# Attention and expert kernel: score pairs as a stream, each side operation behind one pair alone

## The reference

```python
def attn(x, wq, wk, wv, wo):                         # layer 1, 16 heads, d = 8
    Q, K, V = rope(heads(x @ wq.T)), rope(heads(x @ wk.T)), heads(x @ wv.T)
    p = softmax(where(causal, Q @ K.T / sqrt(8), -inf))
    return merge(p @ V) @ wo.T

def ffn(x):                                          # layer 2
    x = x + msa(ln1(x))                              # full attention
    z = ln2(x)
    e = argmax(z @ gate_w + gate_b)
    return x + gelu(z @ w1[e]) @ w2[e]

x = layernorm(x + attn(x)); x = layernorm(x + ffn(x))
```

## Time and profile before

| what | value |
|---|---|
| median of three runs | 973.14 us |
| the profiled execution, its own time | 974.19 us |
| its span, first to last instruction | 972.4 us |
| PE busy, matmuls | 847.0 us, 87% |
| PE busy, weight loads | 371.3 us, 38% |
| ACT busy | 779.5 us, 80% |
| DVE busy | 326.8 us, 34% |
| POOL busy | 223.4 us, 23% |
| granted TensorE clock, mean | 0.935 |
| from the first to the last exponential | 41.9 to 873.6 us |

### The profile page before, as it was taken

How to read it: one execution, slowest core, us unless ns; L and a number is a source line. 1 busy time by engine, 2 the same in 40 slices (tenths; PEclk the granted TensorE clock), 3 DMA queues, 4 the chain that set the end, 5 groups by cost and what they waited for, 6 DMA issues and landing times.

```text
span 972.4 us, 24141 instructions
## 1 busy us (share of the span) xinstructions
PE 847.0 (87%) x9744; PEld 371.3 (38%) x9744; DVE 326.8 (34%) x957; ACT 779.5 (80%) x901; POOL 223.4 (23%) x359
## 2 busy tenths in 40 slices
PE   5689998999999999999989999889999899992261
PEld 2334434344443444333434434434444334442031
DVE  3712614311421034210323322533331633325562
ACT  2468788899999999999989989889989799890340
POOL 4741211111111100000032342033431313321253
PEclk9788999999999999999999999999999999996575
DMA  7975210201110434500100002010000000000101
GB/s 264 274 217 140 88 45 2 88 1 46 45 45 1 101 75 134 172 1 2 45 29 2 2 2 67 7 39 2 3 13 18 29 12 2 2 13 16 38 1 38
DMA packets 34355, 51.58 MB, mean 53 GB/s; under 512 B 4032, under 2 KB 14656, under 8 KB 34240
## 3 DMA queue, kind: packets, MB, share of 16 engines
q1 hardware_dynamic: 32704, 46.30, 16.6%
q0 software_dynamic: 1536, 3.67, 1.2%
HBM read 29.12 MB, written 20.84 MB: 51 GB/s over the span
## 4 chain that ended last, share of the span: by engine, by line
PE 75%; DVE 9%; ACT 7%; issue 4%; DMA 2%; POOL 1%; POOLq 0%; another core or an unknown queue 0%; ACTq 0%; SPq 0%; DVEq 0%
PE ps L447 70%; ACT probs L820 6%; PE ps L452 3%; PE ps L695 2%; ACT squares_blockdiag L857 1%; DVE ln_stats L1010 1%; DVE ln_newton L1003 1%; DMA y_sorted<-early_late 1%; DMA z_rows<-y_sorted,slot_numbers 1%; POOL z_rows L960 1%; DVE squares_blockdiag L1282 1%; DVE ln_newton L1005 0%; DVE ln_newton L1004 0%; DVE z_rows L1019 0%
## 5 line engine op out<-in xcount | busy, mean ns | idle before, releaser
L820 ACT ACTIVATE probs<-ps 128x1024 f32<-128x1024 f32 (+3 forms) x832 | 741.6, 1004 | 87.3 <-PE ps L447 79.6
L447 PE MATMUL ps<-probs,values 128*9 128x256 f32 (+1 forms) x6528 | 438.4, 382 | 1.9 <-DVE q_rotated L1142 1.6
L447 PE MATMUL ps<-query_rows,key_rows 32*128 32x512 f32 (+3 forms) x1664 | 304.4, 491 | 30.7 <-ACT probs L820 26.9
L447 PEld LDWEIGHTS ps<-probs,values 128*9 128x9 f32 x6528 | 144.4, 91 | 192.2 <-issue 92.0
L447 PEld LDWEIGHTS ps<-query_rows,key_rows 32*128 32x128 f32 x1664 | 127.2, 185 | 234.9 <-ACT probs L820 121.2
L919 POOL TENSOR_SCALAR_AFFINE_SELECT probs<-probs 128x256 f32<-128x256 f32 x128 | 53.9, 423 | 246.6 <-ACT probs L820 242.8
L953 POOL COPY parts<-early_late 128x512 f32 x72 | 45.4, 668 | 155.4 <-PE ps L447 155.4
L1142 DVE COPY q_rotated<-ps 128x512 f32<-128x512 f32 x30 | 20.7, 691 | 143.3 <-PE ps L447 127.1
L932 POOL DMA_INDIRECT z_sorted<-z_rows,slot_numbers x16 | 15.7, 981 | 220.9 <-DVE slot_numbers L1272 217.2
L949 POOL COPY parts<-parts 128x512 f32 x72 | 48.0, 710 | 55.7 <-PE ps L447 50.6
L887 ACT ACTIVATE parts<-parts 128x512 f32 x24 | 15.1, 629 | 49.9 <-DVE slot_numbers L1277 28.1
(11 more groups left out here) (155 smaller groups left out, 533.5 us busy)
## 6 DMA issues: line engine op xcount, KB each, us to landing
k_scratch<-parts SPq DMA_DIRECT2D x16, 512.0 KB, 3.8
q_scratch<-parts SPq DMA_DIRECT2D x16, 512.0 KB, 5.1
query_rows<-q_scratch SPq DMA_DIRECT2D x32, 256.0 KB, 5.2
key_rows<-k_scratch SPq DMA_DIRECT2D x20, 256.0 KB, 4.8
key_rows<-k_scratch SPq DMA_DIRECT2D x16, 192.0 KB, 4.3
parts<-in_w SPq DMA_DIRECT2D x1, 2048.0 KB, 8.3
early_late<-in_w SPq DMA_DIRECT2D x8, 256.0 KB, 7.2
early_late<-z_sorted SPq DMA_DIRECT2D x4, 384.0 KB, 3.1
```

The source lines that it names most:

```text
L447: return nc.tensor.matmul(out, l, r, start=start, stop=stop, skip_group_check=True)
L820: nc.scalar.activation(Pr[:, t % 2, 2 * p:2 * p + 2, lo:BLK], score_banks(t, p)[:, :, lo:BLK], ACT.Exp, bias=-SHIFT[r["a"]], scale=SCALE). ...
```

## The change

**The order on PE.** `scores` sends one pair instead of two, and `run` counts pairs since the last interruption (`since`). After two pairs the values of all pairs up to three behind the newest are sent (`late_values`), as before. A side operation now comes as soon as one pair has been sent since the last interruption, ahead of the values, and sets the count back to zero. So one pair of scores stands alone ahead of every side operation, and the values that would have followed it come behind the next two pairs. A turn and the step's side operation, where both fall on one step, still stand together.

**The tables.** The experts' up operations move from steps 26, 32, ..., 56 to 24, 30, ..., 54 (and the tanh with them), their turns from 5 to 4 steps behind the up operation, the down operations stay at 7, so the last down operation of a block moves from step 63 to 61. The sorted rows are turned at 21 and 22 instead of 24 and 25, the output projection comes at 6 instead of 7, and the projections of block (2, 0) start at 15 instead of 13. On DVE the copy of a run's sums is due at `end + 1.5` instead of `end + 1`, and one `due(17)` is gone.

```diff
-UP_AT = (26, 32, 38, 44, 50, 56)
-SORTED_AT = (24, 25)
+UP_AT = (24, 30, 36, 42, 48, 54)
+SORTED_AT = (21, 22)
-    (13, 14, 16, 18, 20, 22, (25, 26, 29, 30)),
+    (15, 16, 18, 20, 22, 23, (25, 26, 29, 30)),
-IN_SHADE = side_order(UP_AT, 5, 7)
+IN_SHADE = side_order(UP_AT, 4, 7)
...
+            late = []
+            def late_values(newest):
+                closed = False
+                while late and 2 * late[0][0]["t"] + late[0][1] <= newest - 3:
+                    step, p = late[0]
+                    if closed and step["start"] and p == 0 and newest <= 2 * step["t"] + 3:
+                        break
+                    values(step, p)
+                    closed = step["stop"] and p == 1
+                    late.pop(0)
...
-                    scores(step)
...
-                    if n >= 2:
-                        values(mine[n - 2], 1)
-                        values(mine[n - 1], 0)
...
-                    for f in side.get(pos, ()):
-                        f()
+                    for p in range(2):
+                        scores(step, p)
+                        late.append((step, p))
+                        since += 1
+                        if since == 1 and due:
+                            if turning:
+                                turn(old, next((c[1:] for c in reversed(freed) if c[0] < pos), None))
+                            for f in side.get(pos, ()):
+                                f()
+                            since, due = 0, False
...
+                        if since == 2:
+                            late_values(2 * step["t"] + p)
+                            since = 0
...
-                    events.append((end + 1, lambda r=r: evac(r)))
+                    events.append((end + 1.5, lambda r=r: evac(r)))
...
-                    due(17)
```

More of the change, by code:

```diff
@@ L588, in general, with scores @@
                     pe.wait_ge(s["gen_unit"], (qb + 1) * units)
-            def scores(step):
+            def scores(step, p):
                 r, t = step["r"], step["t"]
[L593 to L601, removed]
+                if 2 * t + p:
+                    pe.wait_ge(exp, 2 * t + p)
+                for hh in range(2):
+                    rows = slice((2 * p + hh) * ROWS, (2 * p + hh + 1) * ROWS)
+                    last = mm(score_banks(t, p)[:, hh, step["lo"]:BLK],
+                              KAv[rows, r["g"], step["kt"] * P:(step["kt"] + 1) * P],
+                              QAv[rows, r["qb"] % 2, r["g"], step["lo"]:BLK])
+                last.then_inc(S_set, 1)
             def values(step, p):
@@ L708, in _ @@
             side_op = dict(sorted=m_sorted_turn, up=m_up, turn=m_hid_turn, down=m_down)
-            def run(r, side, freed, old):
-                mine = [run_step(r, n) for n in range(r["k1"] - r["k0"])]
-                keys_there(r)
-                for n, step in enumerate(mine):
-                    pos = r["at"] + n
-                    scores(step)
[L717 to L723, removed]
-                    if n >= 2:
-                        values(mine[n - 2], 1)
-                        values(mine[n - 1], 0)
[L727 to L730, removed]
-                    for f in side.get(pos, ()):
-                        f()
-                return mine
+            late = []
@@ new lines, in late_values, with run @@
+            def late_values(newest):
[7 more added lines that the diff above has]
+                    late.pop(0)
+            def run(r, side, freed, old, since):
+                keys_there(r)
+                for n in range(r["k1"] - r["k0"]):
+                    step, pos = run_step(r, n), r["at"] + n
+                    turning = n == TURN_STEP and old is not None and old["closes"]
+                    due = turning or pos in side
+                    for p in range(2):
[8 more added lines that the diff above has]
+                            since, due = 0, False
+                        if n == TURN_STEP and r["last"] and p == 1:
+                            late_values(2 * step["t"] + p)
+                            general(r["a"], r["qb"], step["t"] + 1)
+                            since = 0
+                        if since == 2:
+                            late_values(2 * step["t"] + p)
+                            since = 0
+                return since
@@ L790, in _ @@
                 pe.wait_ge(A[1][name], NB)
-            mine = None
+            old, since = None, 0
             for a in (1, 2):
@@ L796, in _ @@
                     for r in runs_in(a, qb):
[L797 to L800, removed]
+                        since = run(r, side, freed, old, since)
+                        old = r
+            late_values(2 * (old["t0"] + S // P) + 2)
             turn(RUNS[-1], None)
```

4 lines of the change are left out of this document (2 added, 2 removed).

## The result

The changed kernel takes 1042.13 us, median of 4 runs (1036.43 to 1044.92), against 974.14 for the kernel before: a ratio of 1.0681, 95% interval 1.0637 to 1.0725. The forecast was 1011, with a range to 1032. The sign was right, the size was not: 68 us came where 37 were worked out.

What follows compares the result with a forecast made beforehand. ACT's exponentials set the pace, with PE having 0.4 us a step to spare. 88.2 us of new losses less 51.0 gone made 37 us slower than 974.2, forecast 1011; range 992 to 1025, with the third rival 990 to 1032.

Steps and rivals of the forecast that it cites:

- 66 waits behind side operations: ACT waits of 0.25 to 0.7 us in blocks (1, 1) to (2, 3), 26.8 us together, forecast to go away.
- steps 51, 34, 10: ACT idleness at these steps, 6.4, 3.7 and 2.8 us in all, forecast to go away.
- the tail: Behind attention: the fetch of rows comes 4.3 us earlier, so 3.9 us of waiting are won.
- the copy of the sums on DVE: Copies moved behind other DVE work in blocks (1, 3) and (1, 1): 5.6 us lost, elsewhere nothing.
- The third rival: Copies of the sums late at most run ends, eight more at 2.8 us each: 1032 us, chance 0.15.
- The lone place: Side operation behind one pair of scores delays values: ACT idles 0.25, loses 0.35 us, 108 times, 37.8 us.
- The double places: Two side operations on neighbouring steps, one pair between, no values: 25 places, 19.3 plus 25.5 us lost.
- up and down places: Eight double places where an up and a down operation meet: 2.31 us idle, 2.41 lost each, 19.3 us.
- The first rival: PE catches up, lone side operations are hidden, only double places cost: 972 us, chance 0.08.
- the second (the stream gains): Rival: side operations fill PE's wait between scores, only the waits that go away count: 922 us, chance 0.04.
- the late add: Behind attention, DVE's add of fetched rows waits for its DMA until 884.29; forecast to go, winning 3.9 us.

Runs made afterwards that it cites:

- the three sets: Follow-up measurements, four kernels per set, each set on its own chip beside the kernel before, which took 960.35, 959.31 and 959.36 us.
- the stream alone: The kernel before with only the new order on PE, old tables and early copies of the sums: 1020.09 us, ratio 1.0636.

## Why the prediction was wrong in size

The terms, beside what the three sets give for them:

| term | forecast, us | measured, us |
|---|---|---|
| lone and double places (37.8 + 19.3 + 25.5), less the 66 waits behind side operations (26.8 and 66 x 0.1) | +49.2 | +53.1 (999.27 - 946.13) |
| tables: steps 51, 34, 10 (12.9 and 0.8 of restarts), the tail (3.9) | -17.6 | -14.2 (946.13 - 960.35) |
| late copies of the sums | +5.6 | +36 (1035.36 - 999.27); alone +33.6 |
| sum | +37 | +75 (76.0 beside before in one set; 68 on the first chip) |

**The step that failed** is "the copy of the sums on DVE", in its sentence "Elsewhere `end + 1.5` alters the order on DVE by a copy that has slack, and I cost it at nothing". The term was sized at 5.6 us with bounds 0 and 7; it is 34 us in the old order, and 36 (38 by the ratios) in the new. Three things were wrong in it.
- I counted places where the copy passed items of the projections, two of them, and did not follow `due(17)` in blocks (2, 2) and (2, 3). There the copy goes from ahead of a LayerNorm of over 7 us to behind it, in a stretch where the new run's values are needed at once. The cover that I named, that values are sent a group later, hides nothing that the runs show: the late copies cost 36 us with it and 33.6 in the old order, without it.
- In the other places I priced the delay of the values, not what is lost in all: in the changed kernel there are 13 waits of PE (3 before, 4 with early copies), not two.
- I had no price for the clock. After these waits PE ran at half clock, and at half clock PE, not ACT, sets the pace: in the 20.5 us of block (1, 1) PE is busy 19.4 us and ACT 48%, against 90% over attention before. Early copies take 60 us off the time at half clock in attention. That, at 0.90 - 0.55 of a share (0.55 for the two half-clock stretches of blocks (1, 1) and (2, 3), 18.7 of 34.2 us), is an estimate of 21 us (15 without the 17 us of block (1, 0)), and the idle times of ACT on the third steps of runs fall by 18 (29.8 to 11.8); the sum, 33 to 39, is near the 36 measured. The two parts were not measured by themselves, and part of the idleness at low clock can be in both.

The third rival named this mechanism, copies late at run ends, with eight places at 2.8 us and a chance of 0.15; it ended at 1032. It had the right direction, and neither the LayerNorm nor the clock.

**What was right.** The lone place: 99 of 108 such places show idleness of ACT in the kernel with early copies, 46.5 us in all where the working gives 108 x 0.25 = 27, since they hold older waits too: in the kernel with the tables alone the same exponentials idle some 27 us. The double places: 25 with 47.5 us of idleness, against 42.3 in the forecast (44.8 with restarts) and some 15 behind the same places with the tables alone; of the eight up and down places seven stand at 2.40 or 2.41 and one at 1.92. Without the late copies the working gives ACT 84.3 + 69.3 - 39.7 = 113.9 us of waits (69.3 is 27 + 8 x 2.31 + 17 x 1.40), and the kernel with early copies has 111.9.

That many of these waits are for values four pairs back and not for scores is shown from two sides, by a third step of `probs` and by sending the values first, each worth 30 us once the copies are early. It is not all of the stream's price: 23 us stay with the one cure and 29 with the other, beside the old order with the same tables and buffer, and most of them are open. (Two slips in the working change nothing: 3 x 0.917 - 0.5 is 2.25, not 2.26, and the 0.05 in the permit of a+2 has no row.) The first rival (lone operations hidden) and the second (the stream gains) are both out: the stream alone costs 53 to 60 us.

The tables' gain came at four fifths of its size. Of its tail nothing is seen in the tables' run: behind attention 99.4 us against 98.8 before. In the changed kernel, on the first chip, it is 97.1, and the late add is gone; it then waits for the output projection instead:

```profile
949.45 0.69 DVE L1182 TENSOR_TENSOR w_attn<-x_rows,ps 128x512 f32<-128x512 f32 x1 [2.17 <-PE ps L447]
950.18 0.69 DVE L1330 TENSOR_TENSOR x_rows<-x_rows,z_rows 128x512 f32<-128x512 f32 x1
```

The sentence of the Trainium skill that I held to, in "Perfetto Trace Analysis", section "Optimization Strategy", is borne out: a gap that kept coming back on the engine that should be full was a buffer too few (the third step of `probs` is worth 11 us in the old order and 31 in the new). The measure of PE's headroom in the Trainium skill's same page, section "Identifying the Most-Contended Engine", its weight-load share, would have said the opposite, and 38% before and after shows nothing of the 68 us.

## What to carry to other kernels

When a due time moves by half a step, list for every place what it passes in its queue, fixed code between two calls as much as other items, and who waits for the moved operation; "it has slack" needs a number at each place. A side operation sent ahead of work that frees a buffer costs what the buffer lacks, even where the engine has a fifth of its time to spare (0.4 of 1.83 us a step): send what frees first. And if the stall is on PE, time at half clock can follow, here 3 to 20 us behind one and the same wait, so price the stall and the stretch behind it: late copies of 0.7 us, 11 waits of PE of 19.9 us together, cost 33.6.

## What was not expected of the hardware

**The clock after short stalls.** In the changed kernel the wait of PE of 3.48 us at 114 to 117.6 was followed by 0.50 of full clock for 20.5 us, and waits of 2.20 and 1.83 in block (2, 3) went with 13.7:

```profile
830.10:843.80 13.70, 11.37 (x76) 4.07 (x76) 4.38 (x7) 8.89 (x10) 2.83 (x6) 0.50 0.17 49
```

The stall does not set how long this lasts. In the second profile of the changed kernel the same wait, 3.47 us up to 125.88, was followed by 0.50 for 2.8 us more and then by full clock:

```profile
125.90:128.60 2.70, 2.70 (x26) 0.82 (x26) 0.00 (x0) 1.62 (x2) 0.00 (x0) 0.50 0.87 323
128.70:146.00 17.30, 16.08 (x181) 7.60 (x185) 5.35 (x12) 13.41 (x18) 3.27 (x8) 1.00 0.01 2
```

Block (1, 1) took 74.1 us there, and 77.3 in the first profile. What ends a low stretch no run here shows.

**DVE slowed beside POOL.** The last operation of the LayerNorm, four instructions, takes 1.11 us in a quiet place (662.76 above), and in the changed kernel 5.36 while POOL copies expert weights; in its list of durations the longest single one is 4044 ns against a median of 344:

```profile
827.91 5.36 DVE L1032 TENSOR_SCALAR x_rows<-x_rows,ln_meanvar,ln_newton 128x128 f32<-128x128 f32 x4
...
828.43 2.28 POOL L962 COPY parts<-parts 128x512 f32 x4
830.66 1.72 POOL L966 COPY parts<-early_late 128x512 f32 x3
```

```profile
L1032 DVE TENSOR_SCALAR x_rows<-x_rows,ln_meanvar,ln_newton x32: 333/344/4044, 95.5 to 1035.2; 128x128 f32<-128x128 f32 x32
```

POOL's four copies of the first row take 2.28 us, as four of them do in the trace of before (2.27 at 635.64), and DVE's instruction is the one that is stretched. It happened in blocks (2, 2) and (2, 3) just where the late copy stood behind it, and so lengthened its wait. That POOL's copies are the cause is argued from their times alone; no run took them away.

**The chip.** The kernel before took 974.14 us on the first chip and 959.31 to 960.35 on the three others, and the changed kernel 1042.13 on the first and 1035.36 on one of the others.
